# A transformer block on one core: the first output half's copy and the layer norm of the next chunk stand at other places in their engines' order

## What is computed

```python
def attn(x):                         # 16 heads of 32
    Q, K, V = proj(Wq, bq), proj(Wk, bk), proj(Wv, bv)
    Q = Q * cos + _rotate_half(Q) * sin
    K = K * cos + _rotate_half(K) * sin
    scores = jnp.einsum('bhqd,bhkd->bhqk', Q, K) / scale
    scores = jnp.where(causal, scores, -jnp.inf)
    out = jnp.einsum('bhqk,bhkd->bhqd', jax.nn.softmax(scores), V)
    return out.transpose(0, 2, 1, 3).reshape(B, S, H) @ Wo.T + bo

def ffn(x):                          # 1408 inner features, ternary weights
    return ((silu(x @ gate_w.T * gate_s) * (x @ up_w.T * up_s)) @ down_w.T) * down_s

x = x + attn(layernorm(x))
x = x + ffn(layernorm(x))
```

## Time and profile before

| | us |
|---|---|
| median of 3 runs | 768.98 |
| lowest, highest | 768.7, 772.01 |
| profiled execution, its own time | 772.27 |
| its span in the trace | 770.6 |
| projections, to about | 160 |
| attention, to about | 471 |
| output projection and feed-forward | the rest |
| mean granted clock of TensorE | 0.997 of full speed |

### The profile page before, as it was taken

The page is one execution under the profiler, slowest core; times in us unless marked ns, Lnnn a source line. Parts: engine busy times, 40 slices in busy tenths (PEclk is TensorE's granted clock), DMA queues, the critical chain, the costliest instruction groups (busy, mean ns, idle before and its releaser), DMA issues.

```text
span 770.6 us, 10665 instructions
## 1 busy us (share of the span) xinstructions
PE 740.3 (96%) x3563; PEld 540.8 (70%) x3563; DVE 437.1 (57%) x1103; ACT 303.1 (39%) x641; POOL 245.6 (32%) x224
## 2 busy tenths in 40 slices
PE   7998999989999999999999989999999999999996
PEld 7786888765555555555555546787788888888885
DVE  7868493987777767777777726783325114315112
ACT  3231222255555555555555563223332223223221
POOL 0724161502114141414141416832223223223223
PEclk9999999999999999999999999999999999999999
DMA  8584659645656666666566554680001001001001
GB/s 279 210 280 166 219 202 298 257 134 153 155 157 184 157 174 157 166 155 182 157 181 157 141 158 136 223 353 0 1 1 55 0 1 54 0 0 56 0 1 57
DMA packets 54318, 104.39 MB, mean 135 GB/s; under 512 B 14820, under 2 KB 18404, under 8 KB 53748
## 3 DMA queue, kind: packets, MB, share of 16 engines
q1 hardware_dynamic: 54264, 103.72, 44.0%
HBM read 69.62 MB, written 38.21 MB: 140 GB/s over the span
## 4 chain that ended last, share of the span: by engine, by line
PE 75%; DVE 6%; ACT 5%; issue 5%; DMA 5%; POOL 2%; SPq 1%; DVEq 0%; POOLq 0%; ACTq 0%
PE ps L1096 31%; PE ps L1235 17%; PE ps L1311 9%; PE ps L1121 8%; PE ps L1214 8%; ACT p L679 4%; DMA x_st<-in_x 2%; PE ps L1088 1%; ACT o_raw L686 1%; DMA q_st<-neg_max_T 1%; POOL hid_lo L592 1%; DMA w_st<-in_wk 1%; DVE stats L770 1%; DVE xn L785 1%; DMA rec_l<-rec_rows 1%
## 5 line engine op out<-in xcount | busy, mean ns | idle before, releaser
L679 ACT ACTIVATE p<-ps 128x384 f32<-128x384 f32 (+3 forms) x384 | 162.5, 487 | 127.3 <-PE ps L1214 126.8
L842 DVE CUSTOM_DVE_ANT_0 masked<-ps,mask_qk 128x512 bf16<-128x512 f32 (+1 forms) x240 | 114.3, 502 | 77.3 <-PE ps L1121 76.2
L1235 PE MATMUL ps<-p,v_slot 128*64 128x512 f32 (+3 forms) x768 | 137.3, 493 | 7.7 <-ACT o_raw L686 7.6
L1214 PE MATMUL ps<-q_st,k_st 99*128 99x384 f32 (+2 forms) x384 | 134.8, 369 | 2.0 <-DMA q_st<-neg_max_T 1.1
L1121 PE MATMUL ps<-k_st,q_st 96*128 96x512 f32 (+2 forms) x384 | 130.8, 362 | 1.5 <-DVE row_max L842 1.3
L1047 DVE SCALAR_TENSOR_TENSOR hid<-ps,us_sb,silu 128x512 f32<-128x512 f32 x44 | 33.0, 750 | 165.2 <-PE ps L1096 159.5
L592 POOL TENSOR_TENSOR hid_lo<-hid,hid_hi 128x512 fp32r<-128x512 f32 x44 | 56.8, 1290 | 173.0 <-ACT hid_hi L757 173.0
L1235 PEld LDWEIGHTS ps<-p,v_slot 128*64 128x64 f32 x768 | 53.0, 136 | 80.8 <-issue 55.6
L561 POOL TENSOR_SCALAR_AFFINE_SELECT p<-p 128x512 f32<-128x512 f32 x64 | 41.0, 641 | 214.3 <-ACT p L679 214.3
L1121 PEld LDWEIGHTS ps<-k_st,q_st 96*128 96x128 f32 x384 | 72.2, 189 | 31.3 <-issue 21.8
L1214 PEld LDWEIGHTS ps<-q_st,k_st 99*128 99x128 f32 x384 | 72.2, 189 | 20.7 <-ACT p L679 8.8
(11 more groups left out here) (119 smaller groups left out, 1075.1 us busy)
## 6 DMA issues: line engine op xcount, KB each, us to landing
qk_scratch<-st_hi SPq DMA_DIRECT2D x32, 512.0 KB, 3.8
q_st<-qk_scratch SPq DMA_DIRECT2D x32, 384.0 KB, 4.1
k_st<-qk_scratch SPq DMA_DIRECT2D x32, 384.0 KB, 5.2
flag_st<-in_ffn SPq DMA_DIRECT2D x32, 264.0 KB, 2.8
ffn_copy<-in_ffn SPq DMA_DIRECT2D x32, 264.0 KB, 3.3
qk_scratch<-st_lo SPq DMA_DIRECT2D x16, 512.0 KB, 3.7
o_T<-o_raw SPq DMA_DIRECT2D x32, 128.0 KB, 4.1
rec_l<-rec_rows SPq DMA_DIRECT2D x32, 128.0 KB, 3.4
```

What stands on the lines that cost most here:

```text
L679: act.activation(p32[:, at:at + q0 + w - keep], ps[:, ST_BANK + i % ST_RING, keep - q0:w], ACT.Exp, scale=SCALE).then_inc(exp_done, 1)
L842: ins = dve.tensor_tensor_reduce((masked_a if u < 2 else masked)[:, s_before(i) % 2, col:col + kept], scores, mask_qk[:, 512 - kept:512], ...
L1214: pe.matmul(ps[:, ST_BANK + i % ST_RING, 0:w], k_st[0:K_ALL, slot, kt * P:(kt + 1) * P], q_st[0:K_ALL, slot, q0:q0 + w], start=True, stop= ...
L1235: ins = pe.matmul(ps[VW * a:VW * (a + 1), o_bank(u, half), q0 - 512 * half:512], v_slot[:, slot, kt, :], p32[:, at:at + n], start=(kt == 0 ...
```

## The change

It moves operations and adds none. In chunks 1 and 2 of the projections the statistics of the next chunk come ahead of `rotate(0)` and the tokens between `rotate(0)` and `rotate(1)` on VectorE; in chunk 0 the statistics come ahead of `weight_lo(3)`. ScalarE's `std_of` moves with them. SyncE loads x of chunk c + 2 during chunk c, ahead of the outputs of p = 3, where it loaded x of chunk c + 1 at the beginning of chunk c. In the attention, half 0 is copied out behind exponential 3, directly behind the piece that its group of products follows.

```diff
             for c in range(N_CH):
-                if 2 <= c + 1 < N_CH:
-                    sp.wait_ge(ln_done, c + 2)
-                    load_x(x_st[:, :, :], c + 1).then_inc(x_in, 16)
...
                 for p in range(4):
+                    if p == 3 and c + 2 < N_CH:
+                        sp.wait_ge(ln_done, c + 3)
+                        load_x(x_st[:, :, :], c + 2).then_inc(x_in, 16)
...
                 if c == 0:
                     weight_hi(4)
+                elif c < N_CH - 1:
+                    std_of(c + 1)
                 high(0)
                 if c == 0:
+                    std_of(1)
                     weight_hi(5)
-                if c < N_CH - 1:
-                    std_of(c + 1)
...
-                    if t % 2 == 0 and t >= 2 and i == PV_AFTER[0][0] + 3:
+                    if t % 2 == 0 and t >= 2 and i == PV_AFTER[0][0]:
                         evacuate_half((t - 2) // 2, 0)
...
+                def next_statistics():
+                    dve.wait_ge(x_in, 16 * (c + 1))
+                    ln_first(c + 1, x_tiles)
+
+                def next_tokens():
+                    dve.wait_ge(t_ps, TJ * (c + 1))
+                    ln_second(c + 1)
+
+                if 0 < c < N_CH - 1:
+                    next_statistics()
                 rotate(0)
                 if c == 0:
+                    next_statistics()
                     weight_lo(3)
-                if c == N_CH - 1:
+                elif c < N_CH - 1:
+                    next_tokens()
+                else:
                     dve.wait_ge(row_max_init, 1)
                     dve.wait_ge(ln_done, N_CH + 1)
-                if c < N_CH - 1:
-                    dve.wait_ge(x_in, 16 * (c + 1))
-                    ln_first(c + 1, x_tiles)
                 rotate(1)
                 low(0)
-                if 0 < c < N_CH - 1:
-                    dve.wait_ge(t_ps, TJ * (c + 1))
-                    ln_second(c + 1)
...
                 if c == 0:
-                    dve.wait_ge(t_ps, TJ)
-                    ln_second(1)
+                    next_tokens()
```

## The result

The changed kernel takes 764.65 us (median of 12 runs, 762.92 to 770.05), the kernel before, measured beside it, 770.82 us (12 runs, 766.91 to 773.29). The ratio is 0.9932, with a 95% interval of 0.9913 to 0.9951: faster by 0.68%, some 5 us. The forecast was 763.5 in a range of 760.5 to 767.5; against the median then shown, 768.98, it asked for a ratio of 0.9928.

A forecast was written before the change was run, and what follows sets the result against it. TensorE was taken to bound the kernel, so only its holes could be won. From the 769.0 us median, -1.6 (chunk 0), -2.9 (chunk 1 without the clock part) and -1.0 (attention) gave 763.5 us, range 760.5 to 767.5.

The forecast's parts named there:

- What bounds: Whole kernel: TensorE is busy 740.3 of 770.6 us, so only its holes can be won.
- Chunk 0, -1.6: Projections, chunk 0: statistics ahead of `weight_lo(3)` end `rotate(1)` at 27.2, wanted at 27.7; the 1.57 us hole goes.
- the later weight remainder: Chunk 0: `weight_lo(3)` comes 0.8 us later; bounds 0 and +0.8 us, taken as 0.
- half the holes: Rival, chunks 0 and 1: holes shrink but do not go, half of 4.5 us stays, 765.7; chance 0.07.
- x, issued 7.6 us earlier at no cost: SyncE: chunk 2's x issued about 42.5 instead of 50.1, landing between 49.1 and 51.6; the outputs it passes cost 0.
- Even the late case fits: Chunk 1: with x at 51.6, `rotate(0)` ends at 57.1, wanted at 57.5; later rotations were also said to be in time.
- the early case: Chunk 1: x lands at 49.1, so statistics end just at 51.9, where `rotate(0)` starts.
- Chunk 1, -4.5 or -2.9: Projections, chunk 1: both holes go, 34.44 instead of 38.93 us, -4.5 us; without the slow clock's part -2.9 us.
- Tokens beside GpSimd: Chunk 1, VectorE: four tokens, 3.66 us beside GpSimd's rotation, priced at 3.7 us; one more microsecond would still fit.
- Attention, -1.0: Even steps: copy of half 0 behind exponential 3 fits ScalarE's idle time, saving 0.07 us a pair over 15 pairs.
- The level of the median: Whole kernel: three runs show two levels; median 769.0 taken to lack the slow clock, 1.6 us, and row-maximum waits, 1.1 us.
- The small overrun: Rival, attention: the copy delays exponential 4; at 0.15 us for 15 pairs +2.2 instead of -1.0, 766.7; chance 0.2.

The follow-up runs named there:

- before_again: The kernel before, unchanged, run again for a second profile: ratio 0.9996 to the kernel before, median 769.91 us.
- copy_twice: The changed kernel with the copy of half 0 made twice in a row, the second waiting for the first: ratio 1.0026 to the kernel before, 772.48 us.
- order_old_x: The changed kernel with SyncE loading x at the old place, behind all of the chunk before: ratio 1.0055 to the kernel before, 774.91 us.
- copy_alone: The kernel before with only the copy of half 0 moved behind exponential 3: ratio 0.9990 to the kernel before, 769.67 us.
- x_alone: The kernel before with only the earlier load of x, VectorE's and ScalarE's order kept: ratio 0.9964 to the kernel before, 766.87 us.
- old_order_rest: The kernel before with early x, chunk 0's statistics moved, both copies directly behind their exponentials, VectorE's old order in chunks 1 and 2: ratio 0.9870, 760.01 us.
- both_halves: The changed kernel with half 1 also copied out early, behind exponential 9 of the odd step: ratio 0.9860 to the kernel before, 759.81 us.
- proj_alone: The changed kernel with the copy of half 0 back behind exponential 6, projections changed: ratio 0.9936 to the kernel before, 766.80 us.

## Why the prediction was right

**What bounds.** TensorE's holes were the only thing to be won. The time went from 770.82 to 764.65, and the three holes in the projections are gone from the trace of the changed kernel.

**Chunk 0, -1.6.** The hole went; `rotate(1)` ended 0.3 us ahead of the forecast in an execution whose first product came 0.5 us later. The forecast had carried over the 1.77 us of `weight_lo(3)`, which stood beside GpSimd's rotation then (from 21.97, the rotation until 22.65); at its new place it began at 22.99, behind the rotation's end at 22.90, and took 1.23. The chunk became 2.2 us shorter in the profiles, since the slower first matmuls behind the hole (1.16 us for four instead of 1.07) and a delay of 0.2 us ahead of the V products went too: a little undersized for executions that have the hole. The prediction took it that all have it; before_again has none. What I had called free, the later weight remainder, was free where it started 0.5 to 1.5 us ahead of GpSimd's, in six of the nine profiled executions with this order (1.19 to 1.23 us); in the other three the two started within 0.1 us of each other, and in two of these it took 3.44 and 3.43 us, and 0.9 us of hole came back. The prediction carried the cases of half the holes at 0.07; this case was not in it.

**x, issued 7.6 us earlier at no cost.** Issued at 42.04 (forecast 42.5), usable at 50.02. No engine waited for the outputs it passed. It was in time, but with less room than the prediction says. "Even the late case fits" is worked out wrongly: 58.3 and 61.0 belong to the early case, and with x at 51.6 `rotate(0)` ends at 57.1, the tokens at 60.8 and `rotate(1)` at 63.5, where 63.0 is wanted. By the trace the limit is 50.02 + 0.33, some 50.4, and not 52.0; the forecast for the landing, 49.1 to 51.6, lay on both sides of it. That x came at 50.02 was luck in part, and in copy_twice it came 0.2 us too late. Whether x gained by passing the other transfers or by the earlier issue alone is not shown: x took 7.98 us here and 9.12 us at the old place in order_old_x, and no run took the later transfers away.

**Chunk 1, -4.5 or -2.9.** 34.46 us against 38.93 in the profiles, to 0.02 us. The 1.6 us between the two figures, the clock's part, is in the runs: the first 12 matmuls behind the third hole took 4.42 us before, at a granted clock of 0.61 (72.44 to 76.86), and 2.82 us in copy_alone, at 1.00 (71.87 to 74.69). But the step that credits the new order on VectorE is wrong in its cause: x_alone and old_order_rest have the same 34.44 with the old order. The prediction took the early load and the new order as one term, -4.5, and did not ask what x alone would do, though the rows gave it: with x at 52 and the hole of chunk 0 still there, the old order would end `rotate(2)` at 69.5 where 70.1 is early enough (x_alone: 68.95, and 69.35).

**Tokens beside GpSimd.** 3.88 us (55.64) instead of 3.66. Two of the four took 1.54 and 1.51 us beside GpSimd's rotation, the other two 0.53; before, two took 1.32 and 1.51 us beside the rotation. So it cost 0.2 us more, and left `rotate(1)` 0.33 us to spare instead of some 0.5.

**Attention, -1.0.** 19.08 instead of 19.13 to 19.16, 0.05 to 0.07 a pair. Right in size, and too small for the clock on the wall: copy_alone 0.999. The room of 0.1 us ahead of exponential 4 was real, as copy_twice shows. The wait of 7.6 us for half 1 stayed, as said; both_halves then showed that it could be had.

**The level of the median.** Here the prediction reasoned badly from three runs. 768.98, 772.01 and 768.7 looked like two levels; the 12 runs beside the result, together with the later ones, fill the stretch from 767 to 774 without such a gap, and the slow clock came in two of four profiles with the hole. So a typical run may give back part of the clock's 1.6 us. That would make the gain larger than 5.5, and the two profiled spans make it 9.4. Of this, 1.7 is the earlier start of chunk 1, 4.5 chunk 1, 0.3 lies from there to the first pair, and 1.9 lies in the 14 pitches, of which 0.8 is the shorter pitch and 1.1 pairs that were held up, in part by row-maximum transfers. The last 1.0 is ahead of the output projection, whose wait for `oT_lo` of 1.1 us is in the first profile of before; it comes and goes (0.9 us in before_again, 0.7 in proj_alone, none in x_alone), so it and the 1.1 are chance. The many runs give 5.2 us, between 3.8 and 6.7. The terms as the profiles measured them, 2.2, 2.6 to 4.5 and 1.0, would make 5.8 to 7.7. That the total came so near to 5.5 is therefore partly luck: too little taken for the clock and for chunk 0, and nothing taken off for executions in which the first hole is absent before or a late weight half brings one back after. This last part is argued, not shown.

**Rivals.** The small overrun did not happen, x was in time by 0.33 us, and the holes went.

## What to carry to other kernels

A transfer that is wanted early should be issued when its buffer comes free, not where its loop begins: issuing it some 8 us earlier, ahead of 2.5 MB of other transfers, was worth the whole of chunk 1, and the reorder of the consumer was worth nothing that could be measured beside it. It cut the room for x from 3.8 us to 0.33, and with the late load the kernel was 4.2 us slower than before, although the moves of chunk 0 and of the copy were in it. A copy out of PSUM belongs directly behind the last thing that its engine does before it would idle, while the products it waits for run; the same copy one exponential later gave back 0.32 of 0.52 us a pair. It paid what TensorE waited for that copy: 0.07 us a pair for half 0, 0.52 for half 1, which had held it for 0.46. Before a gain is credited to several moves together, work out each alone from the same rows.

## What the runs showed of the hardware

A hole of 1.8 us on TensorE was followed by matmuls at the lower clock in two of four profiled executions (0.55 and 0.64 granted) and not in the other two (1.00), with the same code there: chunk 1 took 38.93 and 38.89 us against 37.06 and 37.47. A hole of 5.99 us in order_old_x was followed by it as well (0.50 granted), and those of 1.57, 1.36 and 1.49 us ahead of p = 3 of chunk 0 in before, x_alone and copy_alone were not (1.00).

VectorE's and GpSimd's subtractions that started within 0.1 us of each other did not run side by side at full speed in any of three executions: twice VectorE took 2.2 us longer (3.44 and 3.43 instead of 1.23 us), once GpSimd took 1.1 us longer (3.52 instead of 2.4 us). GpSimd's row starts first in all three, so the recorded starts do not tell which one pays. The 2.2 and 1.1 us stand in the busy time of the longer row, and not as idle time ahead of it.
